# A macaron block on one core: x loaded behind the write of the routing weights, and turned rows written in one DMA of 2 KB lines and read back in four of 512-byte pieces

## What is computed

```python
x = x + 0.5 * _L0_ffn_ref(_layernorm(x), gate_w, gate_b, w13, w2, w13_s, w2_s)
x = x + _L0_attn_ref(_layernorm(x), w_q, w_k, w_v)
x = x + 0.5 * _L0_ffn_ref(_layernorm(x), gate_w, gate_b, w13, w2, w13_s, w2_s)

# _L0_ffn_ref: 16 experts of width 64, 4 of them for each token, and a shared one
scores = jax.nn.sigmoid(xt @ gate_w.T)
_, idx = lax.top_k(scores + gate_b, 4)
w = scores at idx, divided by their sum, times 2.5        # comb: 16 weights a token, 12 of them 0
y = sum over e of comb[:, e] * (silu_and_mul(xt @ w13[e].T) @ w2[e].T)  +  the shared expert

# _L0_attn_ref: one head of 128, rotary positions, causal softmax
q, k, v = x @ w_q.T, x @ w_k.T, x @ w_v.T
attn = softmax(causal(rotate(q) @ rotate(k).T / sqrt(128))) @ v
```

## Time and profile before

| | us |
|---|---|
| median of 3 runs | 840.5 (839.95 to 840.89) |
| the profiled execution: its time | 840.94 |
| its span, from the first to the last instruction | 839.2 |
| PE busy in it | 810.6 |
| DVE, ACT, POOL busy | 717.7, 591.4, 621.9 |

### The profile page before, as it was taken

The page is one execution under the profiler, slowest core; times in us unless marked ns, Lnnn a source line. Parts: engine busy times, 40 slices in busy tenths (PEclk is TensorE's granted clock), DMA queues, the critical chain, the costliest instruction groups (busy, mean ns, idle before and its releaser), DMA issues. The chain is left out here.

```text
span 839.2 us, 15741 instructions
## 1 busy us (share of the span) xinstructions
PE 810.6 (97%) x4022; PEld 649.8 (77%) x4022; DVE 717.7 (86%) x2030; ACT 591.4 (70%) x1491; POOL 621.9 (74%) x560
## 2 busy tenths in 40 slices
PE   8799999999989899999999999999999999999998
PEld 7577777776766677789999999767777777777777
DVE  7889998988978798878888886789998889999986
ACT  5777777776765567766766766677778777787664
POOL 6777777876766568978888896177777877888664
PEclk9999999999999999999999999999999999999999
DMA  7567767666787656353444342466656677766653
GB/s 223 146 172 207 204 187 184 181 179 182 228 253 234 195 159 189 99 156 113 127 125 125 109 113 83 109 177 175 173 174 188 202 196 191 202 175 171 168 141 100
DMA packets 92152, 140.82 MB, mean 168 GB/s; under 512 B 9408, under 2 KB 38704, under 8 KB 91824
## 3 DMA queue, kind: packets, MB, share of 16 engines
q1 hardware_dynamic: 92080, 140.03, 59.7%
HBM read 112.67 MB, written 18.93 MB: 157 GB/s over the span
## 5 line engine op out<-in xcount | busy, mean ns | idle before, releaser
L629 POOL TENSOR_TENSOR h_l<-probT,h_h 128x512 fp32r<-128x512 f32 x254 | 337.6, 1336 | 161.8 <-ACT h_h L853 159.5
L1791 PE MATMUL bank<-xh,w_h 128*128 128x512 f32 x545 | 217.9, 400 | 10.0 <-DVE prob L1309 7.3
L853 ACT ACTIVATE h_h<-probT 128x512 fp32r<-128x512 f32 (+1 forms) x285 | 178.8, 627 | 56.7 <-DVE probT L1319 33.0
L1791 PE MATMUL bank<-xh,w_l 128*128 128x512 f32 x545 | 214.6, 394 | 0.0
L1791 PE MATMUL bank<-xl,w_h 128*128 128x512 f32 x545 | 214.3, 393 | 0.0
L1309 DVE TENSOR_TENSOR prob<-bank,qkT 128x512 f32<-128x512 f32 x252 | 171.7, 681 | 29.0 <-ACT bank L916 18.5
L916 ACT ACTIVATE bank<-bank 128x512 f32<-128x512 f32 x252 | 146.0, 579 | 63.0 <-PE bank L1791 61.5
L1319 DVE TENSOR_TENSOR probT<-prob,bank 128x512 f32<-128x512 f32 x255 | 171.2, 671 | 10.2 <-POOL h_l L629 3.4
L1791 PEld LDWEIGHTS bank<-xh,w_h 128*128 128x128 f32 x545 | 102.6, 188 | 46.9 <-DVE prob L1309 13.9
L1791 PE MATMUL bank<-h_h,w_h 128*128 128x512 f32 (+1 forms) x297 | 118.3, 403 | 7.6 <-POOL h_l L629 6.5
L1791 PEld LDWEIGHTS bank<-xh,w_l 128*128 128x128 f32 x545 | 102.6, 188 | 23.3
(11 more groups left out here) (143 smaller groups left out, 1329.4 us busy)
## 6 DMA issues: line engine op xcount, KB each, us to landing
qkT<-comb_rows SPq DMA_DIRECT2D x190, 256.0 KB, 5.1
qkT<-comb_rows SPq DMA_DIRECT2D x124, 128.0 KB, 3.0
rows<-comb_rows SPq DMA_DIRECT2D x28, 512.0 KB, 7.1
stage<-stage SPq DMA_DIRECT2D x64, 128.0 KB, 2.4
X<-in_x SPq DMA_DIRECT2D x16, 256.0 KB, 7.3
stage<-in_x_t SPq DMA_DIRECT2D x16, 256.0 KB, 7.4
x_t<-stage SPq DMA_DIRECT2D x16, 256.0 KB, 4.5
X<-x_rows SPq DMA_DIRECT2D x8, 512.0 KB, 7.6
```

What stands on the lines that cost most here:

```text
L629: nc.gpsimd.tensor_tensor(lo, f, hi.bitcast(F32), ALU.subtract).then_inc(done, 1)
L853: return nc.scalar.activation(dst, src, ACT.Copy)
L1791: return nc.tensor.matmul(dst, lhsT, rhs, start=start, stop=stop)
```

## The change

There are four edits to what is moved, and two to the order of work on ACT and DVE.

1. The load of x of tile T + 4 is issued directly behind the write of the routing weights, ahead of the wait for its landing.
2. The turned rows of a tile are written in one DMA (128 lines of 2 KB), as they stand on the partitions. They are read back in four DMAs a tile, each 32 partitions by 4 pieces of 512 bytes, which do the reordering.
3. The reading back goes by tile and starts with tile 4 of the loop (tile T - 4 in tile T) where before it went by batch and started with tile 10. Each reading waits for the landing of the one before it (`x_done`). At the seam, tiles 12 and 13 are read ahead of the load of x1 and of the statistics, and 14 and 15 at the end.
4. Mask, cos and sin are loaded in halves in tiles 4 to 9, where before they were loaded whole in tiles 10 to 12.
5. In the opening, tile 0's logits go through ACT like the later ones, and ACT's silu of the logits (`ffn_gsilu`) moves behind the silu of step 0 and a rounding of weights.
6. In tile 13 the second half of batch 0's statistics moves behind the low half of x of tile 15 (`ffn_xl`) and the product of step 8.

```diff
--- before.py
+++ after.py
@@ -90,6 +91,7 @@
 WARM = 16, 5
 G = P // NB
 TURN_DMAS = 16 * NB
+ROW_DMAS = 16 * NB
 TURN_AHEAD = 4
 ROOT_D = float(np.sqrt(np.float32(D)))
 MEAN_SCALE, DEV_SCALE = -1.0 / (D * ROOT_D), 1.0 / ROOT_D
...
@@ -397,7 +399,11 @@
 
         def logitsT_count(T, base):
 
-            return T - (1 if base else 0)
+            return T + (0 if base else 1)
+
+        def turned_count(n):
+
+            return 16 * n if isinstance(n, int) and n <= TILES else 16 * TILES + TURN_DMAS * (n - TILES)
 
         def stats_count(T, base):
 
...
@@ -448,12 +454,14 @@
                 sp.wait_ge(xT_moved[r], 32 * turn)
                 sp.dma_start(xT[r], x_t[:, bass.ds(TILE * T, TILE)]).then_inc(xT_moved[r], 16)
 
-            def comb_rows(T, q, first=0, base=0, ahead=True, swap=None, store_behind=None):
+            def comb_rows(T, q, first=0, base=0, ahead=True, swap=None, store_behind=None, x_tile=None):
 
 
 
                 sp.wait_ge(combT_done, T + 1)
                 sp.dma_start(comb_d[q].rearrange("e (a t) -> a e t", a=NB), combT[q][:]).then_inc(comb_written, 16)
+                if x_tile is not None:
+                    load_x(x_tile, x_tile % 2)
                 sp.wait_ge(comb_written, 16 * (T + 1))
                 src = comb_d[q, 0:NEXP, :].rearrange("(j a) t -> a j t", a=2)
                 for g, (j0, j1) in enumerate(COMB_PAIRS):
...
@@ -476,35 +484,31 @@
                 sp.wait_ge(xr_done, T + 1)
                 sp.dma_start(out_t[:, bass.ds(TILE * (T - TILES), TILE)], xT[r]).then_inc(xT_moved[r], 16)
 
-            def write_turned(n):
-
-                sp.wait_ge(turn_done, n + 1)
-                wait(sp, turn_written, TURN_DMAS * n)
-
             def write_x1_rows(T, src):
 
-                write_turned(T)
+                sp.wait_ge(turn_done, T + 1)
+                wait(sp, turn_written, turned_count(T))
+                sp.dma_start(x1_rows[T], src).then_inc(turn_written, 16)
+
+            def load_x1_rows(T):
+
+                sp.wait_ge(turn_written, turned_count(T + 1))
+                wait(sp, x_done, ROW_DMAS * T)
                 for a in range(NB):
-                    sp.dma_start(x1_rows[bass.ds(T, 1), G * a:G * (a + 1), :].rearrange("t r (i x) -> (t i) r x", i=NB),
-                                 src[:, a * P:(a + 1) * P]).then_inc(turn_written, 16)
-
-            def load_x1_rows(b):
-
-                sp.wait_ge(turn_written, TURN_DMAS * 2 * (b + 1))
-                wait(sp, x_done, 16 * b)
-                sp.dma_start(X[:, QB * b:QB * (b + 1), :].rearrange("p (t k) d -> p t (k d)", t=2),
-                             x1_rows[2 * b:2 * b + 2].rearrange("t p f -> p t f")).then_inc(x_done, 16)
+                    sp.dma_start(X[G * a:G * (a + 1), tile_blocks(T), :],
+                                 x1_rows[T, :, P * a:P * (a + 1)].rearrange("(i r) x -> r i x", i=NB)).then_inc(x_done, 16)
 
             def write_x2(T, src):
 
-                write_turned(T + TILES)
+                sp.wait_ge(turn_done, T + TILES + 1)
+                wait(sp, turn_written, turned_count(T + TILES))
                 for i in range(NB):
                     sp.dma_start(x2_d[G * i:G * (i + 1), bass.ds(TILE * T, TILE)].rearrange("c (a x) -> a c x", a=NB),
                                  src[:, i * P:(i + 1) * P]).then_inc(turn_written, 16)
 
             def load_x2(T, r):
 
-                sp.wait_ge(turn_written, TURN_DMAS * (TILES + T + 1))
+                sp.wait_ge(turn_written, turned_count(TILES + T + 1))
                 wait(sp, xT_loaded, 16 * (T - 2))
                 sp.dma_start(xT[r], x2_d[:, bass.ds(TILE * T, TILE)]).then_inc(xT_loaded, 16)
 
...
@@ -512,23 +516,20 @@
                 comb_rows(0, 0, SPREAD)
                 comb_rows(1, 1)
                 for T in range(2, TILES):
-                    comb_rows(T, T % 2, 0, 0, T + 2 < TILES, 0 if T == TILES - 1 else None, store_x1)
-                    if T + 4 < TILES:
-                        load_x(T + 4, T % 2)
+                    comb_rows(T, T % 2, 0, 0, T + 2 < TILES, 0 if T == TILES - 1 else None, store_x1,
+                              T + 4 if T + 4 < TILES else None)
                     if T + 2 < TILES:
                         sp.wait_ge(turn_done, T - 1)
                         load_xT(T + 2, (T + 2) % RING, (T + 2) // RING)
-                    if T == 10:
-                        load(mask[:], mask_d, rope_loaded)
-                    elif T == 11:
-                        load(cos[:], cos_d, rope_loaded)
-                    elif T == 12:
-                        load(sin[:], sin_d, rope_loaded)
-                    if T >= 10:
-                        load_x1_rows(T - 10)
+                    if T in ROPE_TILES:
+                        dst, src = ((mask, mask_d), (cos, cos_d), (sin, sin_d))[(T - ROPE_TILES[0]) // 2]
+                        half = (slice(None), T % 2) if dst is not mask else (slice(None), slice((M + P) // 2 * (T % 2), (M + P) // 2 * (T % 2 + 1)))
+                        load(dst[half], src[half], rope_loaded)
                     if T == TILES - 1:
                         swap_halves(0, 1)
                     write_x1_rows(T - 2, turned[T % 2])
+                    if T >= NB:
+                        load_x1_rows(T - NB)
                 store_x1(TILES - 2, RING - 2)
                 swap_halves(0, 2)
                 write_x1_rows(TILES - 2, a_turned[0])
...
@@ -576,13 +577,14 @@
                 swap_halves(b + 1, 1)
                 if isinstance(b, int) and b == 0:
                     write_x1_rows(TILES - 1, a_turned[1])
-                    load_x1_rows(B - 2)
+                    load_x1_rows(TILES - 4)
+                    load_x1_rows(TILES - 3)
                     for r in range(RING):
                         sp.wait_ge(xT_moved[r], 32 * TURNS)
                 else:
                     sp.wait_ge(a_xs_done, 2 * b)
                 if isinstance(b, int) and b + TURNED == B:
-                    sp.wait_ge(turn_written, TURN_DMAS * (TILES + 2))
+                    sp.wait_ge(turn_written, turned_count(TILES + 2))
                     sp.dma_start(a_xT, x2_d[:, 0:M]).then_inc(a_xT_loaded, 16)
                 else:
                     sp.dma_start(a_xT, x1_d[:, bass.ds(M * (b + TURNED), M)]).then_inc(a_xT_loaded, 16)
...
@@ -594,7 +596,8 @@
                 attn_rows(b, 1)
                 swap_halves(b + 1, 3)
                 if isinstance(b, int) and b == 0:
-                    load_x1_rows(B - 1)
+                    load_x1_rows(TILES - 2)
+                    load_x1_rows(TILES - 1)
                 if isinstance(b, int) and b >= B - 3:
                     for a in range(2):
                         write_x2(2 * (b - B + 3) + a, a_turned[a])
...
@@ -1016,10 +1019,11 @@
                     opening_xh(base, 0)
                     act.wait_ge(w13_loaded[1], 16)
                     copy(w13_h[:, early[1], :], w13_f[:, early[1], :]).then_inc(w13_hi[1], 1)
-                    ffn_gsilu(base)
+                    ffn_logitsT(base, base)
                     ffn_silu(base, 0, 0)
                     act.wait_ge(w13_loaded[2], 16)
                     copy(w13_h[:, early[2], :], w13_f[:, early[2], :]).then_inc(w13_hi[2], 1)
+                    ffn_gsilu(base)
                     ffn_silu(base, 0, 1)
                     ffn_silu(base, 0, 2)
                     for n in range(NB):
...
@@ -1197,7 +1201,7 @@
 
             def ffn_logits_turn(T, base):
 
-                if isinstance(T, int) and T == base:
+                if base and T == base:
                     dve.wait_ge(logitsT_ready, T + 1)
                     for a in range(NB):
                         ins = nc.vector.transpose(logits[G * a:G * (a + 1), :], bank[0:G, T_BANK, a * P:(a + 1) * P])
...
@@ -1515,19 +1519,19 @@
                             dve.wait_ge(a_neg_shift_done, 1)
                             attn_stats(1)
                         elif j == NB + 1:
-                            dve.wait_ge(x_done, 16 * 2)
+                            dve.wait_ge(x_done, ROW_DMAS * 4)
                         attn_ln(1, j - NB - 1)
-                    if T == TILES - 3 and j in (NB + 1, PAIRS - 1):
-                        if j == NB + 1:
-                            dve.wait_ge(x_done, 16)
-                        attn_ln(0, int(j == PAIRS - 1))
-                        if j == PAIRS - 1:
-                            attn_stats(0)
+                    if T == TILES - 3 and j == NB + 1:
+                        dve.wait_ge(x_done, ROW_DMAS * 2)
+                        attn_ln(0, 0)
                 if t + 2 < TILES:
                     ffn_xl(T + 2, q)
                 if first_batch == 0:
                     attn_item(("xnT", 0), 0, 0, True)
                 ffn_h(T, q, PAIRS)
+                if T == TILES - 3:
+                    attn_ln(0, 1)
+                    attn_stats(0)
 
             def ffn_start():
 
...
@@ -1762,7 +1766,7 @@
                     if first and i == 1:
```

(13 more changed lines are left out.)

## The result

| | before | changed |
|---|---|---|
| median (lowest to highest) of 4 runs each | 840.69 us (839.95 to 844.82) | 830.24 us (829.22 to 831.10) |
| the profiled execution, and its span | 840.94, 839.2 | 829.22, 827.4 |

The ratio is 0.9865, with a 95% interval of 0.983 to 0.9901: the change makes the kernel faster, by 10 us by the medians and 11 by the ratio; the interval spans 8 to 14 us. The forecast was a gain of 6.1 us, to 834.4; the measured time is above the low end of its range by 0.7 us, and 0.9865 x 840.5 = 829.2 is just under it. The direction was right, the size was not.

A forecast was written before the change was run, and what follows sets the result against it. PE, busy 97% of the span, was taken as the bound, gaining only its waits and clock loss. 840.94 - 6.1 - 5.1 - 0.9 - 0.6 + 4.9 + 1.7 = 834.8, or 834.4 against the median; range 829.5 to 839.5.

The forecast's parts named there:

- the size of what the loop could give: Whole kernel: PE can gain only its waits, 28.6 us, and what its clock loses.
- x loaded early: Loop, 60 to 260 us: all ten ACT waits for x go, and with them PE's waits for POOL: -6.1 us.
- Rival D: Loop: only the waits for x go, and 2 us of new ones on xT or rows appear: 836.5 us; chance 0.2.
- One write: Loop's late tiles: the write uses all engines, so DVE-product waits (3.0 + 0.4) and the clock fall (1.7) go: -5.1 us.
- rival C: Turned rows: memory, not engines, sets 87 GB/s, so the write gets no faster: 839.5 us; chance 0.07.
- Four reads a tile: Loop from tile 4: issuing the reads takes 2.0 us a tile, hidden before the next weights: 0; bound +8.
- rival B: Tiles 4 to 9: a backlog in the fuller loop makes the weights late, PE waits for DVE: 842.4 us; chance 0.08.
- Statistics in tile 13: Tile 13: moving 0.85 us of statistics from ahead of xl removes PE's wait of 1.0 us: -0.9 us.
- The opening: Start: DVE's turning ends near 11.8 us, not 12.3, and PE's 3.15 us wait at 29.0 shrinks: -0.6 us.
- The seam: After the loop: reads landing in sequence delay DVE by 4.9 us (+4.9); PE stands 5.7 us, its clock falls (+1.7).
- inside this wait: Seam: POOL's centering for batch 2 comes 2.6 us later, within DVE's wait for the last reads.
- Rival A: Seam: the gains come without its price, as reads land faster or DVE is not held: 827.8 to 830; chance 0.15.

The follow-up runs named there:

- kernel 1: The kernel before with only the load of x moved directly behind the write of the routing weights: 833.55 us, ratio 0.9896.
- kernel 2: The kernel before with only the four writes of turned rows recut, 32 rows outermost instead of 4 blocks, same 512-byte pieces: 831.95 us, ratio 0.9879.
- kernel 4: The changed kernel with the load of x back in its old place, behind the reads of the weights: 838.78 us, ratio 0.9949.
- kernel 7: The changed kernel with the reads of turned rows at the seam spread over places where SP waits anyway: 823.4 us, ratio 0.9768.
- kernel 8: The changed kernel with the seam's reads spread over SP's waits and also the old opening: 823.75 us, ratio 0.9773.
- kernel 9: The changed kernel measured again, with nothing altered: 830.49 us, ratio 0.9852.
- kernel 5: The changed kernel with tile 13's statistics back in their old place, ahead of xl: 830.27 us, ratio 0.9862.
- kernel 6: The changed kernel with the opening of the kernel before: 827.93 us, ratio 0.9826.

## Why the prediction was wrong

**The step that failed: the size of what the loop could give.** The prediction took it from PE's listed waits, "the kernel can gain only what PE waits for: 839.2 - 810.6 = 28.6 us", 6.1 us for x and 5.1 for the write. The mechanisms were those it named: kernel 1 shows the one, kernel 2 the other, kernel 4 the first once more from the other side. In the change tiles 3 to 12 gave 8.5 us and tiles 12 to 15 gave 9.3. PE's timeline of before shows why.

```profile
109.55 0.39 PE L1791 MATMUL bank<-xl,w_h 128*128 128x512 f32 x1
109.77 0.40 PE L1791 MATMUL bank<-xh,w_l 128*128 128x512 f32 x1
110.35 0.51 PE L1791 MATMUL bank<-h_h,w_h 128*128 128x512 f32 x1 [0.18 <-POOL h_l L629]
110.70 0.39 PE L1791 MATMUL bank<-h_h,w_l 128*128 128x512 f32 x1
```

A matmul starts every 0.23 us and is shown 0.39 long, so two overlap by 0.16. Here the next one starts 0.58 after the last, 0.35 late, and the one after it 0.35 on, another 0.12: 0.47 us are lost and 0.18 are listed. A stall that ends within the overlap is not listed at all. Summed over the single matmuls from 60 to 260 us, what the starts lie apart beyond 0.231 us (gaps with more than 0.05 us of it) is 14.3 us in 59 gaps before, where 6.1 are listed, and 3.1 us in 20 gaps after, where none is. The same stretch of the two kernels, first before, then changed:

```profile
100.00:120.00 20.00, 19.77 (x84) 14.92 (x83) 18.12 (x49) 14.81 (x42) 15.09 (x15) 1.00 0.73 192
```

```profile
100.00:120.00 20.00, 19.95 (x87) 15.68 (x86) 18.07 (x51) 15.65 (x43) 15.79 (x15) 1.00 0.84 237
```

Before is busy for 19.77 us of 20 and has three matmuls fewer, 0.69 us of work, with 0.23 us of idle. The trace of before held the right size all the same. Its two neighbouring milestones at 164.47 and 183.06 lie 18.59 us apart, one tile in which PE has no listed wait. Nine tiles at that pace are 167.3 us, 8.5 less than they took, and three are 55.8, 10.2 less; measured 8.5 and 9.3. That is found with the result known, and for this one kernel.

**x loaded early (-6.1; measured -7.7 alone, -8.3 within the change).** In the change all ten waits of ACT for x and all of PE's for POOL went, and nothing became late in their place: right but for the size. Rival D, small new waits on `xT` or rows in the loop, didn't come up: PE has no listed wait from 60 to 260 us. (Its time should read 836.4, 834.4 + 2.)

**One write (-5.1; tiles 12 to 15: -7.1 by the shape alone).** The 4 or 5 engines of the old write, inferred from 0.29 x 16, agree with the 4 to 6 packets under way at once; these packets and kernel 2 refute rival C. "Just the turned rows of one tile" was a misreading: 64 KB of the tail are the write of the weights, issued at 145.13 and landed behind the turned rows. What I hadn't counted is that the slow write also cost 3.6 us in tiles 3 to 12: it holds SP's queue, and so the late load of x is later still. In tiles 9, 10 and 11 of before `X<-in_x` is issued 11.8, 12.1 and 12.9 us behind the weights, in kernel 2 10.1, 10.1 and 10.6, and in these three tiles the 3.6 us are gained.

**Four reads a tile (0).** Taken: 2.0 us to issue four. Measured in the loop (SP, tile 7; then the first load of the next tile's weights at 162.9, so they are hidden):

```profile
156.30 1.80 SPq L498 DMA_DIRECT2D X<-x_rows  x4
```

The term of 0 holds, and rival B with it is out: the slowest of the tiles 4 to 9 takes 18.6 us. But kernel 4 shows how much this rests on the early load.

**Statistics in tile 13 (-0.9; measured -0.2, not to be told from 0 in the time).** The wait of 1.04 us was really removed, and a wait of 0.56 us for `xn`, 14 us later, took about half of its place.

**The opening (-0.6; measured +0.9 to tile 1, +1.4 to tile 3; worth nothing by kernels 7 and 8).** ACT's copy was to let DVE end its turning near 11.8 us and not at 12.3. It ended at 12.1, since DVE now met x of tile 2 1.42 us too early. ACT released PE sooner, PE ran out of work sooner, and then the clock fell. PE's and DVE's timelines of the change:

```profile
17.12 1.10 PE L1820 MATMUL bank<-ident,cos 128*128 128x128 f32 x6 [2.29 <-DVE cos L1580]
...
29.94 0.50 PE L1795 MATMUL bank<-xh,w_h 128*128 128x512 f32 x1 [3.23 <-DVE prob L1313]
```

```profile
10.62 0.87 DVE L1363 BATCH_NORM_STATS2 stats<-X 128x6 f32<-128x128 f32 x4 [1.42 <-DMA X<-in_x]
```

The wait at 29 was to shrink from 3.15; it is 3.23. The profiles of all the kernels tell the price of the order from that of the clock. From the weights of tile 0 to those of tile 1 nine of the eleven take 13.44 to 13.46 us, three with the new opening among them; the two with a fall near 18 us, the first of the change and kernel 9, take 14.56 and 14.65. So 1.1 of the 1.4 us came with that fall. From tile 2 to 3 all five profiles with the new opening take 19.07 to 19.10 us and all six with the old one 18.75 to 18.77: 0.3 us against the new order. Up to the weights of tile 0 the new order is 0.35 us ahead in the mean of the profiles, with spreads of 0.65 and 0.93 us.

**The seam (+4.9 and +1.7; measured +4.6).** SP came late as reckoned, and DVE waits 6.1 us where 5 to 7 were expected: 4.57 more than the 1.52 of before, which is the whole price. DVE, POOL, ACT and PE of the change (answering to the earlier trace rows):

```profile
358.05 0.64 DVE L1182 BATCH_NORM_AGGREGATE mv<-stats 128x2 f32<-128x6 f32 x8 [6.09 <-DMA X<-x_rows]
```

```profile
350.60 1.27 POOL L791 TENSOR_TENSOR xn<-stage,rows 128x512 f32<-128x512 f32 x1 [4.49 <-DMA rows<-stat_rows]
```

```profile
354.53 0.63 ACT L856 ACTIVATE qkT<-rot 128x512 fp32r<-128x512 f32 x1 [3.60 <-POOL rot L806]
355.07 1.06 ACT L856 ACTIVATE probT<-bank 128x512 f32<-128x512 f32 x2
```

```profile
355.70 3.45 PE L1795 MATMUL bank<-stage,probT 128*128 128x128 f32 x16 [2.97 <-ACT probT L856]
...
360.57 0.49 PE L1795 MATMUL bank<-stage,probT 128*128 128x128 f32 x2 [0.55 <-ACT probT L856]
```

Two things were not as forecast. PE stands for 2.97 and 0.55 us and not for 5.7, and it is stopped first through another chain: late statistics, POOL's centering, ACT's rounding of `rot`, and behind it in ACT's order the copy of `probT` that PE needs. I had called POOL's delay "inside this wait"; it is, but it reaches PE by itself. And the clock does fall (0.57 from 356 to 360), but its 1.7 us were counted twice: the slow matmuls run while DVE still waits, until 358.05. PE's next gate comes 360.57 - 358.05 = 2.5 us behind DVE's release, against 372.74 - 369.85 = 2.9 in the earlier trace rows. Rival A asked for a seam without a price, and its time (827.8 to 830) is near the measured one, but not its reason: the price was paid and the loop gave more.

## What to carry to other kernels

Where an engine is busy for 97% and its instructions overlap in the records, size the loss by the pace: the time between two equal places of neighbouring tiles, less that of the quickest tile in the same trace; the listed waits tell who is late, not how much is lost. A queue that waits for a landing is a free place for the next issues; the same reads cost 4.6 us in a row at the seam, and nothing once they were spread over such waits. And of a DMA whose outermost dimension is four, try another cut before anything else.

## What the runs showed of the hardware beyond what was expected

- Cut as 4 blocks outermost, a tile's turned rows and the weights behind them ran for 3 us at 87 GB/s and a share of 0.29; with the rows cut as 32 outermost, in the same 512-byte pieces, nothing of that tail was left. A packet of 512 bytes took 27 ns either way; 4 to 6 were under way at once in the one, up to 18 in the other. One edit of the pattern is worth 1.2% of this kernel (kernel 2).
- A wait's length alone doesn't say whether the granted clock falls. In the first profile of the changed kernel it fell to 0.54 behind a wait of 2.29 us and stayed at 1.00 behind one of 3.23; in the second profile of the same code it fell behind 1.7 (0.53) and behind 3.2 (0.55); in that of before it fell at neither. Kernel 7 has the waits of that second profile, 1.68 and 3.18 us, and its clock fell behind the second only. What decides it stays open.
- A fall of the clock costs only what is on the path: 4 us at 0.57 at the seam added nothing that can be found, while the one near 18 us goes with 1.1 us more from tile 0 to tile 1. From tile 1 to tile 2 the three profiles without a fall near 28 us take 17.89 to 18.02 us, the five with a short one 18.39 to 18.62, and the three in which the clock stayed down for twice as long (kernels 5, 6 and 9) 19.50 to 19.62.
